# Starting the tile stage of a routed expert layer while Pool still scatters the last list entries

## What is computed

```python
h = _layernorm(x) * (1 + ca) + sa
x = x + ga * attn(h)              # layernorm, projections k, v, r, a scan over time, Wo
h = _layernorm(x) * (1 + cb) + sb
x = x + gb * ffn(h)

def _moe_group(x2, router_w, wg, wu, wd, top_k):      # ffn: the mean of two such groups, top_k = 2
    scores = softmax(x2 @ router_w)                   # 32 experts in each group
    w, e = top_k(scores, 2)
    y = (silu(x2 @ wg[e]) * (x2 @ wu[e])) @ wd[e]     # 512 -> 256 -> 512
    return sum of w * y over the two chosen experts
```

## Time and profile before

| | us |
|---|---|
| median of 3 runs | 5163.3 (5159.52 to 5163.87) |
| the profiled execution | 5175.09 |
| its span, from the first to the last instruction | 5173.3 |
| PE busy | 4644.2 (90%) |
| DVE busy | 3124.7 (60%) |
| POOL busy | 2858.7 (55%) |
| ACT busy | 1625.5 (31%) |
| the chain that ended last, by engine | PE 32%, DMA 20%, issue 4%, POOL 2% |
| of it, adding rows into `out` by DMA | 19% |

### The profile page before, as it was taken

How to read it: one execution, slowest core, us unless ns; L and a number is a source line. 1 busy time by engine, 2 the same in 40 slices (tenths; PEclk the granted TensorE clock), 3 DMA queues, 4 the chain that set the end, 5 groups by cost and what they waited for, 6 DMA issues and landing times.

```text
span 5173.3 us, 89076 instructions
## 1 busy us (share of the span) xinstructions
PE 4644.2 (90%) x22649; PEld 3825.1 (74%) x22649; DVE 3124.7 (60%) x6155; ACT 1625.5 (31%) x4045; POOL 2858.7 (55%) x2301
## 2 busy tenths in 40 slices
PE   6989898989998885689889987998999999999998
PEld 4777777777777774467677776777878888888886
DVE  6898889889888885444344443454434444444443
ACT  2334333343443342123222332332222222222222
POOL 2566777776667775344344443554545555555554
PEclk8999999999999997799999998999999999999999
DMA  5545454545454452799999998999899899898887
GB/s 219 175 148 172 142 177 145 167 151 173 155 169 151 152 163 93 267 302 287 311 306 299 301 287 287 285 319 300 211 266 262 219 258 259 223 253 218 216 230 190
DMA packets 413885, 1152.42 MB, mean 223 GB/s; under 512 B 57057, under 2 KB 57058, under 8 KB 394930
## 3 DMA queue, kind: packets, MB, share of 16 engines
q0 software_dynamic: 182512, 454.27, 36.6%
q1 hardware_dynamic: 189634, 544.27, 29.2%
q10 hardware_dynamic: 41472, 151.01, 7.7%
HBM read 719.35 MB, written 463.57 MB: 229 GB/s over the span
## 4 chain that ended last, share of the span: by engine, by line
PE 32%; DMA 20%; issue 4%; POOL 2%; DVE 1%; POOLq 1%; SPq 0%; DVEq 0%; ACT 0%; ACTq 0%
DMA out<-c_yo,c_idx 19%; PE ps L1284 9%; PE ps L1286 9%; PE ps L1285 9%; PE ps L1293 3%; PE ps L1312 1%; POOL out L1275 1%; POOL c_xg L1244 1%; DMA c_wt<-wsp_d 1%; DVE c_yo L1528 1%; POOLq L1267 0%; DVE c_xl L1516 0%; DMA wsp_d<-c_stg 0%; DVE c_hTl L1521 0%; POOL c_lists L1256 0%
## 5 line engine op out<-in xcount | busy, mean ns | idle before, releaser
L1275 POOL DMA_INDIRECT out<-c_yo,c_idx x576 | 919.4, 1596 | 1067.5 <-DMA out<-c_yo,c_idx 617.8
L1284 PE MATMUL ps<-c_wt,c_xh 128*128 128x512 f32 x2304 | 967.6, 420 | 46.3 <-issue 22.9
L1286 PE MATMUL ps<-c_wt,c_xl 128*128 128x512 f32 x2304 | 911.1, 395 | 0.0
L1285 PE MATMUL ps<-c_wt,c_xh 128*128 128x512 f32 x2304 | 906.8, 394 | 0.0
L1528 DVE SCALAR_TENSOR_TENSOR c_yo<-ps,c_wc,c_xg 128x512 f32<-128x512 f32 x576 | 432.5, 751 | 730.2 <-DMA out<-c_yo,c_idx 471.0
L1244 POOL DMA_INDIRECT c_xg<-h2g_d,c_idx x576 | 569.7, 989 | 513.5 <-DVE c_yo L1528 403.2
L1512 DVE TENSOR_TENSOR c_hh<-ps,c_sil 128x256 f32<-128x256 f32 x576 | 243.8, 423 | 823.6 <-ACT c_sil L1364 756.2
L1369 ACT CAST c_xh<-ps 128x512 fp32r<-128x512 f32 x576 | 337.7, 586 | 1091.4 <-PE ps L1293 1005.0
L431 PE MATMUL ps<-xTh,wTh 128*128 128x512 f32 x1536 | 622.0, 405 | 61.7 <-DVE xTl L798 57.8
L692 POOL DMA_INDIRECT list_d<-pairs,sidx x512 | 556.0, 1086 | 215.5 <-issue 127.5
L1284 PE MATMUL ps<-c_wt,c_hTh 128*128 128x512 f32 x1152 | 468.1, 406 | 159.8 <-DVE c_hTl L1521 145.9
(11 more groups left out here) (196 smaller groups left out, 8032.3 us busy)
## 6 DMA issues: line engine op xcount, KB each, us to landing
c_wt<-wsp_d SPq DMA_DIRECT2D x69, 2048.0 KB
c_wt<-wsp_d SPq DMA_DIRECT2D x69, 1024.0 KB
sraw<-wex SPq DMA_DIRECT2D x194, 256.0 KB
wsp_d<-shigh SPq DMA_DIRECT2D x192, 256.0 KB
wsp_d<-sraw SPq DMA_DIRECT2D x192, 256.0 KB
c_stg<-wex ACTq DMA_DIRECT2D x96, 512.0 KB
wsp_d<-c_sgh ACTq DMA_DIRECT2D x96, 512.0 KB
wsp_d<-c_stg ACTq DMA_DIRECT2D x96, 512.0 KB
```

Source lines behind the costliest of these rows:

```text
L1275: nc.gpsimd.indirect_dma_start(out=out, out_offset=bass.IndirectOffsetOnAxis(ap=idx[:, n:n + 1], axis=0), in_=yo[:, n % 4, :], in_offset=N ...
L1284: nc.tensor.matmul(o, lh, rh, start=first, stop=False)
L1285: nc.tensor.matmul(o, lh, rl, start=False, stop=False)
L1286: return nc.tensor.matmul(o, ll, rh, start=False, stop=last)
```

## The change

At the end of `stage_a`, TensorE does `ranks(B,0)` ahead of `output(B,0)`, and VectorE `place(B,-2)` ahead of `residual(B,-1)`. Pool does three of the next-to-last step's scatters ahead of the reciprocal root and 13 behind it. The last step's 16 scatters move over the barrier to the start of `stage_c`; `sidx` and `pairs` therefore live in memory that both stages hold. At the start of `stage_c` the iota of `slot` is gone (made in the setup), that of `odd` is replaced by two memsets on VectorE, and that of `before` stands behind the list gathers. The list gathers wait for the scatters. The transposes of `eidx` and the copy to `c_eord` come before the lists instead of behind them, `c_idx` is made before `c_tmax`, and the last operations of `c_must` come behind the first two `xlo`.

```diff
@@ build @@
+        slot = whole.enter_context(nc.sbuf_tensor("slot", [P, COLS], U32))
+        sidx = whole.enter_context(nc.sbuf_tensor("sidx", [P, 2, TJ * G * 2], U32))
+        pairs = whole.enter_context(nc.sbuf_tensor("pairs", [P, 2, TJ * G * 2, 2], F32))
@@ stage_a, tensor @@
+            ranks(B, 0)
             output(B, 0)
-            ranks(B, 0)
             back(B, 0)
@@ stage_a, gpsimd @@
+            scatter(B, -2, 0, 3)
             rstd(b_var, vab, h2_ready, rsb, b_rstd, B, -1)
-            scatter(B, -2, 0, 16)
-            scatter(B, -1, 0, 16)
+            scatter(B, -2, 3, 16)
             pool.wait_ge(scattered[0], 2 * B * 16 * 16)
-            pool.wait_ge(scattered[1], 2 * B * 16 * 16)
+            pool.wait_ge(scattered[1], (2 * B - 1) * 16 * 16)
@@ stage_a, vector @@
             topk(B, -2)
+            place(B, -2)
             residual(B, -1)
-            place(B, -2)
             modulate(B, -1)
@@ setup, gpsimd @@
+            g.iota(L["slot"][:], [[P, L["COLS"]]], base=0, channel_multiplier=1)
@@ stage_c, gpsimd @@
-            nc.gpsimd.iota(slot[:], ...).then_inc(numbered, 1)
-            nc.gpsimd.iota(before[:], ...).then_inc(numbered, 1)
-            nc.gpsimd.iota(odd[:], ...).then_inc(numbered, 1)
+            for i in range(sidx.shape[2]):
+                nc.gpsimd.indirect_dma_start(
+                    out=list_d, out_offset=bass.IndirectOffsetOnAxis(ap=sidx[:, 1, i:i + 1], axis=0),
+                    in_=pairs[:, 1, i, :], in_offset=None).then_inc(placed, 16)
             list_rows = list_d.rearrange("(r n) c -> r (n c)", n=P)
             pool.wait_ge(listed, 1)
+            pool.wait_ge(placed, 16 * sidx.shape[2])
             for c in range(COLS):
                 ...
+            nc.gpsimd.iota(before[:], ...).then_inc(numbered, 1)
@@ stage_c, tensor @@
                     gate_up(it, s)
+                    if first and s == 0:
+                        pe.wait_ge(t_read, 1)
...
+            pe.wait_ge(listed, 1)
+            for c in range(COLS):
+                last = nc.tensor.transpose(ps[0:1, 4 + c // 4, ...], eidx[:, c:c + 1], ident[:])
+            last.then_inc(t_done, 1)
             pe.wait_ge(l_in, 16 * COLS)
...
-            for c in range(COLS):
-                last = nc.tensor.transpose(ps[0:1, 4 + c // 4, ...], eidx[:, c:c + 1], ident[:])
-            last.then_inc(t_done, 1)
...
             pe.wait_ge(t_exp, 1)
-            pe.wait_ge(t_must, 1)
@@ stage_c, vector: find_lists @@
-                dve.wait_ge(numbered, 1)
...
                 V.tensor_copy(rowu[:], row[:]).then_inc(listed, 1)
+                V.memset(pair[:, :, 0:1], 0.0)
+                link(V.memset(pair[:, :, 1:2], 1.0 * P))
+                dve.wait_ge(t_done, 1)
+                V.tensor_copy(eord[:], flat(2)[0:1, :]).then_inc(t_exp, 1)
@@ stage_c, vector: keep_lists and keep_order @@
+                dve.wait_ge(t_done, 2)
+                link(V.scalar_tensor_tensor(out=odd[:], in0=flat(0), scalar=1.0 * N, in1=odd[:],
+                                            op0=ALU.is_ge, op1=ALU.mult))
+                V.tensor_tensor(idx[:], flat(0), odd[:], ALU.add).then_inc(t_idx, 1)
                 dve.wait_ge(l_in, 16 * COLS)
...
                 V.tensor_reduce(tmax[:], cand[:], AX_X, ALU.max).then_inc(t_max, 1)
-                dve.wait_ge(t_done, 1)
-                dve.wait_ge(numbered, 3)
-                link(V.scalar_tensor_tensor(out=odd[:], ...))
-                V.tensor_tensor(idx[:], flat(0), odd[:], ALU.add).then_inc(t_idx, 1)
-                dve.wait_ge(t_done, 2)
+                dve.wait_ge(t_done, 3)
                 V.tensor_copy(ws[:], flat(1)).then_inc(t_ws, 1)
...
-                V.tensor_copy(eord[:], flat(2)[0:1, :]).then_inc(t_exp, 1)
...
-                V.tensor_tensor(meet[:, 0, 0:n1], emin[:, 1:], emax[:, 0:n1], ALU.is_le)
+                V.tensor_tensor(meet[:, 0, 0:n1], emin[:, 1:], emax[:, 0:n1], ALU.is_le).then_inc(t_read, 1)
+
+            def keep_order():
                 link(V.tensor_tensor(meet[:, 1, 0:n1], emin[:, 0:n1], emax[:, 1:], ALU.is_le))
+                dve.wait_ge(t_read, 1)
...
-                dve.wait_ge(numbered, 2)
+                dve.wait_ge(numbered, 1)
...
             xlo(0, 1)
+            keep_order()
             turn(0, first=True, splitting=True)
```

More of the change, by code:

```diff
@@ L155, in stage_a @@
     ps, ident, base, first_entry = L["ps"], L["ident"], L["base"], L["first_entry"]
+    sidx, pairs = L["sidx"], L["pairs"]
     xf, mod_d, h2g_d, list_d, wsp_d = L["xf"], L["mod_d"], L["h2g_d"], L["list_d"], L["wsp_d"]
@@ L189, in stage_a @@
         shigh = sb("shigh", [P, 2, C], F32R)
-        sidx = sb("sidx", [P, 2, R * 2], U32)
-        pairs = sb("pairs", [P, 2, R * 2, 2])
         rws = sb("rws", [P, KC, GE])
@@ L1119, in stage_c @@
     ps, ident, base, first_entry = L["ps"], L["ident"], L["base"], L["first_entry"]
+    slot, sidx, pairs = L["slot"], L["sidx"], L["pairs"]
     h2g_d, list_d, wsp_d, wex, out = L["h2g_d"], L["list_d"], L["wsp_d"], L["wex"][1], L["out"]
@@ L1138, in stage_c @@
         ones = sb("ones", [P, 1])
-        slot = sb("slot", [P, COLS], U32)
         sgrp = sb("sgrp", [P, COLS])
@@ L1178, in stage_c @@
         numbered, chain, listed, l_in = sem("numbered"), sem("chain"), sem("listed"), sem("l_in")
+        placed, t_read = sem("placed"), sem("t_read")
         t_done, t_idx, t_ws, t_exp = sem("t_done"), sem("t_idx"), sem("t_ws"), sem("t_exp")
@@ L1258, in _ @@
                     in_offset=bass.IndirectOffsetOnAxis(ap=rowu[:, c:c + 1], axis=0)).then_inc(l_in, 16)
+            nc.gpsimd.iota(before[:], [[16, COLS * P // 2], [0, 2]], base=0, channel_multiplier=0,
+                           allow_small_or_imprecise_dtypes=True).then_inc(numbered, 1)
             pool.wait_ge(t_idx, 1)
@@ L1332, in turn @@
                     turn_h(it, s)
+            pe.wait_ge(listed, 1)
+            for c in range(COLS):
+                last = nc.tensor.transpose(ps[0:1, 4 + c // 4, c % 4 * P:(c % 4 + 1) * P], eidx[:, c:c + 1], ident[:])
+            last.then_inc(t_done, 1)
             pe.wait_ge(l_in, 16 * COLS)
@@ L1339, in _ @@
             for c in range(COLS):
-                last = nc.tensor.transpose(ps[0:1, 4 + c // 4, c % 4 * P:(c % 4 + 1) * P], eidx[:, c:c + 1], ident[:])
-            last.then_inc(t_done, 1)
-            for c in range(COLS):
                 nc.tensor.transpose(ps[0:1, 6 + c // 4, c % 4 * P:(c % 4 + 1) * P], lists[:, c, 0, 0:1], ident[:])
@@ L1345, in _ @@
             for c in range(COLS):
-                o = ps[0:1, 5, (1 + c) * P:(2 + c) * P] if c < 3 else ps[0:1, 7, (c - 2) * P:(c - 1) * P]
+                o = ps[0:1, 7, (1 + c) * P:(2 + c) * P] if c < 3 else ps[0:1, 1, (c - 1) * P:c * P]
                 last = nc.tensor.transpose(o, tmax[:, c:c + 1], ident[:])
@@ L1428, in _, with flat @@
             n = [0]
+            emin = cand[0:1].rearrange("p c n -> p (c n)")
+            emax = odd[0:1]
+            meet = lists[0:1].rearrange("p c n k -> p (c n k)").rearrange("p (a n) -> p a n", a=2)
+            n1 = COLS * P - 1
+            def flat(k):
+                return ps[:, 2 * k:2 * k + 2, :].rearrange("p a b -> p (a b)")[:, 0:COLS * P]
             def link(ins):
@@ L1474, in find_lists @@
                 V.tensor_copy(rowu[:], row[:]).then_inc(listed, 1)
+                pair = odd[:].rearrange("p (n two) -> p n two", two=2)
+                V.memset(pair[:, :, 0:1], 0.0)
+                link(V.memset(pair[:, :, 1:2], 1.0 * P))
+                dve.wait_ge(t_done, 1)
+                V.tensor_copy(eord[:], flat(2)[0:1, :]).then_inc(t_exp, 1)
             def keep_lists():
-                def flat(k):
-                    return ps[:, 2 * k:2 * k + 2, :].rearrange("p a b -> p (a b)")[:, 0:COLS * P]
+                dve.wait_ge(t_done, 2)
+                link(V.scalar_tensor_tensor(out=odd[:], in0=flat(0), scalar=1.0 * N, in1=odd[:],
+                                            op0=ALU.is_ge, op1=ALU.mult))
+                V.tensor_tensor(idx[:], flat(0), odd[:], ALU.add).then_inc(t_idx, 1)
                 dve.wait_ge(l_in, 16 * COLS)
@@ L1483, in keep_lists @@
                 V.tensor_reduce(tmax[:], cand[:], AX_X, ALU.max).then_inc(t_max, 1)
-                dve.wait_ge(t_done, 1)
-                dve.wait_ge(numbered, 3)
-                link(V.scalar_tensor_tensor(out=odd[:], in0=flat(0), scalar=1.0 * N, in1=odd[:],
-                                            op0=ALU.is_ge, op1=ALU.mult))
-                V.tensor_tensor(idx[:], flat(0), odd[:], ALU.add).then_inc(t_idx, 1)
-                dve.wait_ge(t_done, 2)
+                dve.wait_ge(t_done, 3)
                 V.tensor_copy(ws[:], flat(1)).then_inc(t_ws, 1)
-                emin = cand[0:1].rearrange("p c n -> p (c n)")
-                emax = odd[0:1]
-                meet = lists[0:1].rearrange("p c n k -> p (c n k)").rearrange("p (a n) -> p a n", a=2)
                 dve.wait_ge(t_idx, 1)
```

(13 more changed lines are left out.)

5 lines of the change are left out of this document (removed).

## The result

The changed kernel took **5138.75 us** (median of 7 runs, 5133.25 to 5144.41) against 5163.87 for the kernel before beside it (7 runs, 5152.26 to 5178.27): a ratio of 0.9949, 95% interval [0.9935, 0.9963]. That is a gain of 26 us with 19 to 34 allowed. I had forecast 5121, a gain of 42.5, with a range of 5110 to 5140. The direction is right and the time lies inside the range, near its slow end; of the forecast gain six tenths came.

What follows compares the result with a forecast made beforehand. No single engine was taken to bound the whole; the seam between stages was. Gains of 23.4 us at slot 0 and 19.1 from weight waits up to slot 4 made 42.5, off the 5163.3 median: 5121, range 5110 to 5140.

Steps and rivals of the forecast that it cites:

- two rivals that did not come: Seam: entries held behind the weights (5137 us, 12%), and VectorE locking Pool's descriptor port (5128 us, 9%).
- part 4: Scatters and list gathers beside weight loads: last landing 1 us later, list gathers 10.3 us, lists in at 2077.7.
- my case: The main forecast at the seam: gain 42.5 us at slot 4, 5121 us, own range 5115 to 5130, 66%.
- the first rival: Scatters beside weights: each takes 4.5 us, slot 4 near 2126.7, gain 26, total 5137 us; chance 12%.
- Part 1: First stage's end: place(-2) moved into VectorE's idle time takes 2.45 us off the path, sidx at 2043.6.
- it moves as a block: Chain from L858 to sidx, logits included: keeps its length, at half TensorE's clock in both cases.
- Part 2: Barrier: Pool's drain ends near 2037 under VectorE's chain, 6 us to spare, else 5.29 us return; stage start 2045.0.
- The port: Scatters beside find_lists: VectorE locks Pool's descriptor port, lists 8 us later, gain 35, 5128 us; skill's figures make 30; 9%.
- The same work in the same order: Behind slot 4: the work is unchanged, so no backlog from the seam eats the gain.
- the dense stretch takes back: Stretch with DMA over 0.9 busy: DMA sets the pace, earlier start partly waited away; at half, 5142 us; 8%.

Runs made afterwards that it cites:

- weights-late run: Changed kernel with SP waiting for the lists before its first weight load; 5157.51 us (9 runs), ratio 0.9973 to the kernel before.
- the repeat: The changed kernel run again, text unchanged; 5136.47 us (4 runs), ratio 0.993 to the kernel before, 5173.23 on that chip.
- r10: Changed kernel with one unused tensor, 128 bytes a partition, that moves every buffer of both stages; 5121.56 us (4 runs), ratio 0.9936 to the kernel before.
- two-slot run: Changed kernel with weights of slots 0 and 1 issued at once, those of slots 2 and 3 after the lists; 5150.36 us (6 runs), ratio 0.9966.
- r9: Kernel before with 384 bytes a partition of unused tensors, putting the tile stage's buffers at the changed kernel's addresses; 5162.3 us (10 runs), ratio 1.0016.
- r7: Changed kernel with 12 already met waits ahead of ranks in TensorE's program; 5135.93 us (4 runs), ratio 0.9942 to the kernel before.
- r11: Kernel before with only TensorE's ranks(B,0) moved ahead of output(B,0); 5150.76 us (10 runs), ratio 0.9998.

## Why the prediction was right, and where its size was off

**The mechanism held at every step that I named.** No Pool drain stood between `sidx` and the barrier, VectorE's first operation came at 2034.3 (forecast 2045, which less the 8.2 us of this execution is 2036.8), no long operation in `find_lists`, weights 10.3 us into the stage (forecast 9.9), no wait for `c_wt` in slots 1 to 3, and from slot 0 to slot 4 20.3 us (forecast 20.1; 39.2 before). The weights-late run shows from the other side that loading them early is worth the price that the lists pay. That the time lies within the range is in part luck: its slow end was there for two rivals that did not come, the 8 us that addresses cost stood in no term, and the logits' 3.5 us, which I had not forecast either, made up for some of what the lists lost.

**The seam, step by step** (forecast against measured):

| | forecast | measured | gain against forecast |
|---|---|---|---|
| output's matmul to the end of `sidx` | 46.9 | 43.9 | +3.0 |
| end of `sidx` to the stage's first operation | 1.4 | 1.9 | -0.5 |
| stage start to list gathers | 22.4 | 28.5 | -6.1 |
| list gathers to lists in | 10.3 | 12.1 | -1.8 |
| lists in to slot 0 | 12.6 | 11.3 | +1.3 |
| slot 0 to slot 4 | 20.1 | 20.3 | -0.2 |
| **sum** | | | **-4.3** |

- *The step that failed is part 4's price*: "only the landing is later, by 1 us". I priced entries beside weights by packets, one for one, at 0.55 us a round, as the row gathers had it in the earlier trace rows. The changed kernel moved 173 small packets beside 296 of the weights in 10 us, not one for one. The landing came 6.0 us later than unloaded and the list gathers 4.2 us: 10.2 where I had 1.0 + 2.5. Another 0.8 is that unloaded, too, the list gathers start 2.0 us behind the last issue's end, where I took 1.2. (The 2 us of latency in my 10.3 for the list gathers stood in no row.) The truth lies between my case and the first rival, that entries crawl behind the weights; that rival's own mark, scatters ending with the weights and slot 4 at 2126.7, did not come.
- *Part 1 was too small*: "it moves as a block" was wrong for the logits, which came 3.5 us quicker with the new tail. `place`'s 2.45 us came as worked out. "At half TensorE's clock in both cases" was so in this pair (0.50), but not in the repeat, where the 32 matmuls took 3.75 us; the copy came at the same time all the same.
- *Part 2*: the cover held with 4 us to spare, not 6, and the r10 run shows the price that I named for its loss being paid in part: 2.8 us. Pool's drain took 3.99 us in the changed kernel, not 5.29.
- *The port* did not show. The scatters beside `find_lists` took 0.96 us each and started 1.26 apart. The Trainium skill, SBUF — State Buffer, section Who interferes with whom, states that beside a VectorE instruction in a two-port mode whichever of the two issues second is blocked for the whole of the other's instruction. VectorE's instructions in `find_lists` take 0.06 to 0.55 us, so by that rule a scatter would wait for some tenths of a microsecond (an estimate), and my 2.5 us for each took the page's 3100 ns over to operations too short for it. The trace shows not even the tenths, but for one scatter of 1.28 us in the two-slot run and one of 1.29 in r10.

**Behind slot 4.** "The same work in the same order" was true, yet not at the same addresses. Moving `sidx`, `pairs` and `slot` shifted the tile stage's buffers, and by r9 that alone costs 0.16% (8 us, interval 3 to 13). 38.2 less 8 is 30. The three comparisons of the changed kernel's order at its own addresses gave 26, 36 and 30 us (the third is r7). So of a forecast some 12 us too large 4 were lost at the seam and 8 by addresses; the first comparison's 26 lies 4 lower still, within its interval of 19 to 34. That leaves little for what "the dense stretch takes back" named, an earlier start waited away on DMA; Pool's waits for landed adds from 2200 to 4000 did not grow (423.2 against the earlier trace rows's 436.7; 383 to 450 in all executions). But single executions differ by up to 16 us between slots 3 and 256 with no pattern by kernel (1450 to 1466 us), so a give-back of a few us there can't be excluded.

**Left open**: why the logits' time hangs on the tail's order; why the addresses set the pace; why three variants of the changed kernel lose 6 to 15 us more in the runs than at slot 3; and the 7 us of the next section.

## What to carry to other kernels

Moving a load ahead of small transfers is worth it when the load is what the consumer waits for last, but price the small transfers by an unloaded run beside a loaded one: here the last 8-byte entries landed 8 us behind their issue beside weight loads instead of 2. A stage's order can't be costed by its instructions alone when the edit moves a buffer from one pool to another: pad the old kernel to the new addresses and time that before crediting or blaming the new order. And where a wait is hidden under a chain, say what happens when the chain gets quicker: the cover, 4 us as measured, was gone as soon as the logits took 5 us instead of 10.

## What the runs showed of the hardware that was not expected

- **Addresses.** In the kernel before, 384 bytes of unused room cost 8 us (1.0016 [1.0005, 1.0026]) at 4.794 us a slot, and 404 bytes left the pace at 4.774; in the changed kernel 128 bytes more took it from 4.794 to 4.779.
- **A late end of the logits.** In the ten executions before r9 ScalarE's copy came 3.7 to 7.5 us behind the start of the last recorded logits matmul, released by nothing that the profile names (`<-remote`); on the chip of r9 to r11 it came 0.3 to 0.5 us behind. That is up to 7 us in one chain, with nothing in the kernels to account for it.
- **Small transfers beside large ones.** Unloaded, a scatter of 128 entries had landed 2.0 us behind its issue; with weight loads under way 7.5 to 8.0. Five list gathers took 7.9 and 12.1 us. The loads pay too: from 2046 to 2056 a weight packet took 0.55 us (101.1% of 16 engines' 10 us by 296), in the earlier trace rows, beside row gathers, 0.41 (74.2% by 290), and DMA moved 330 GB/s in place of 421 (3.15 and 1.06 MB in 10 us). From 2055 to 2063 it was 302, from 2066 to 2076, behind the scatters, 419.
- **Pool's drain** at the barrier goes with what the stage's end leaves to Pool: 5.29 us in all six executions that end with the last step's scatters, 3.99 in all seven without them, and it is long even though the waits for all landings are met.
